# Four graph layers: from eight barriered blocks to one program per engine

## What is computed

```python
h = x
h = h + multi_head_graph_attention(h, adj)      # layer 0, 8 heads, masked softmax
h = layernorm(h); h = h + elu(graph_attention(h, adj))   # layer 1, 1 head
h = layernorm(h); h = h + relu(adj_sum(gated(h)))        # layer 2, relational
h = layernorm(h); h = h + attention(h, adj) @ Wo.T + bo  # layer 3, 4 heads
out = layernorm(h)

def layernorm(x, eps=1e-05):
    m = mean(x); v = var(x)
    return (x - m) / sqrt(v + eps)
```

## Time and profile before

| | |
|---|---|
| time, median of 3 runs | 827.31 (826.11 to 828.08) |
| profiled execution | 827.92, of which span 822.1 |
| busy share of the span | PE 85%, VectorE 75%, ScalarE 68%, GpSimd 49% |
| mean granted TensorE clock | 0.955 of full speed |
| layers, first to last work | 20 to 293, 300 to 433, 440 to 546, 551 to 814 |
| table loads from layer 0 on | 7, of 1.28 each |
| GpSimd's loads of the adjacency | median 3.0 from issue to landing |

### The profile page before, as it was taken

One profiled execution on the slowest core, in us unless ns is written; L12 is line 12 of the kernel. 1 busy time (PEld: TensorE's weight loads), 2 busy tenths in 40 slices (PEclk: granted clock), 3 DMA queues, 4 the chain that ended last, 5 costly groups with the idle time before them and its releaser, 6 DMA issues. The chain is left out here.

```text
span 822.1 us, 26183 instructions
## 1 busy us (share of the span) xinstructions
PE 700.0 (85%) x8450; PEld 517.3 (63%) x8482; DVE 616.0 (75%) x1758; ACT 560.4 (68%) x1266; POOL 399.7 (49%) x615
## 2 busy tenths in 40 slices
PE   5589999999998728999964999959999999999982
PEld 3366666666666416676744999946666666666751
DVE  4158878888788727999984788874777787778765
ACT  1346666656665449999955999945777777877871
POOL 0447787787778422545431111103455545545540
PEclk9999999999999959999986999978999999999995
DMA  1514333333332011232311333310222222222211
GB/s 47 147 47 98 79 83 96 94 72 90 96 71 46 16 27 21 38 38 32 39 13 52 91 81 86 90 28 11 48 46 51 57 45 53 56 57 45 53 47 39
DMA packets 34919, 47.76 MB, mean 58 GB/s; under 512 B 4394, under 2 KB 18484, under 8 KB 34868
## 3 DMA queue, kind: packets, MB, share of 16 engines
q0 software_dynamic: 18576, 21.01, 16.1%
q1 hardware_dynamic: 16292, 26.10, 10.1%
HBM read 51.33 MB, written 8.39 MB: 73 GB/s over the span
## 5 line engine op out<-in xcount | busy, mean ns | idle before, releaser
L490 DVE SCALAR_TENSOR_TENSOR pp<-banks,floor,adj 128x1024 f32<-128x1024 f32 x128 | 157.3, 1249 | 2.9 <-PE banks L585 2.5
L1113 POOL TENSOR_TENSOR pp<-pp,adj 128x512 f32<-128x512 f32 x64 | 73.5, 1166 | 121.5 <-ACT pp L1154 121.5
L416 ACT COPY rows<-banks 128x640 bf16<-128x640 bf16 x64 | 44.3, 692 | 69.4 <-PE banks L562 69.2
L1154 ACT ACTIVATE pp<-banks,nobound 128x512 f32<-128x512 f32 x128 | 81.5, 696 | 3.8 <-PE banks L1336 2.1
L585 PE MATMUL banks<-pp,yv 128*17 128x128 f32 x2048 | 82.5, 280 | 1.5 <-DVE pp L490 1.4
L716 POOL TENSOR_TENSOR yres<-oo,x 128x512 f32 (+1 forms) x32 | 40.8, 1275 | 67.6 <-DVE oo L821 67.6
L572 PE MATMUL banks<-rows 32*128 32x128 bf16 x1024 | 51.5, 219 | 22.2 <-DVE pp L490 20.6
L1032 PE MATMUL banks<-w2b,xt 128*128 128x256 f32 x256 | 61.8, 385 | 0.0
L340 POOL TENSOR_TENSOR yv<-wh,yv 128x512 f32<-128x512 f32 x32 | 35.2, 1099 | 52.1 <-ACT yv L409 52.1
L916 POOL DMA_DIRECT2D adj<-in_adj x32 | 17.0, 533 | 85.1 <-ACT sq L951 74.1
L421 ACT COPY ot<-banks 128x512 f32<-128x512 f32 x64 | 37.4, 584 | 29.4 <-PE banks L585 29.4
(11 more groups left out here) (219 smaller groups left out, 1953.7 us busy)
## 6 DMA issues: line engine op xcount, KB each, us to landing
adj<-in_adjt POOLq DMA_DIRECT2D x96, 128.0 KB, 3.0
xt<-in_xt SPq DMA_DIRECT2D x32, 256.0 KB, 3.8
x<-in_x SPq DMA_DIRECT2D x32, 256.0 KB, 3.2
adj<-in_adj POOLq DMA_DIRECT2D x32, 256.0 KB, 3.0
out_ngd<-yres SPq DMA_DIRECT2D x32, 256.0 KB
w3q<-in_wq SPq DMA_DIRECT2D x1, 64.0 KB, 1.8
w3k<-in_wk SPq DMA_DIRECT2D x1, 64.0 KB, 2.2
ident<-in_ident SPq DMA_DIRECT2D x1, 64.0 KB
```

Source lines behind the costliest of these rows:

```text
L416: nc.scalar.copy(rows[:, slot % 2, a, :], R[:, 0:5 * N]).then_inc(s["rw"], 1)
L490: nc.vector.scalar_tensor_tensor(pp[:, g], S[g % 2][:, :].rearrange("p (h n) -> p h n", n=N), floor[:, slot:slot + 1], adj[:, slot, g:g + ...
L1113: nc.gpsimd.tensor_tensor(pp[:, slot % 2, h], pp[:, slot % 2, h], adj[:, slot], ALU.mult).then_inc(s["pm"], 1)
L1154: nc.scalar.activation(pp[:, slot % 2, h], S[h][:, :], ACT.Exp, bias=k["nobound"][:, :], scale=SCALE).then_inc(s["p"], 1)
```

## The change

The functions of the four layers and `verdict` no longer open blocks. They return their programs (`Programs`), and a new function `layers` joins them into one program per engine inside one block and one phase. Semaphores are then taken for all of it: 135 in one clearing at the end, where each layer had its own (42, 23, 14 and 35) and each `row_statistics` and `verdict` 3.

`row_statistics` is gone. A class `Rows` does its work in two portions: portion 0 is graphs 0 to 119 (the first 30 portions of the batch), portion 1 the last 8 graphs. `variance` is the first seven VectorE operations as before. `roots` replaces square root and reciprocal by exp(-0.5 ln v) on ScalarE, and `refine` follows on VectorE with one Newton step and `nmr`. A layer's normalisations wait for `done` 1, those of its last two portions for `done` 2.

In layer 0 the table that holds both logarithm and exponential is named at the start, and it serves layer 1 too; it is named again at the end of layer 2 instead of at the start of layer 3.

Buffers of neighbouring layers lie in different parts of one area (`Plan`, 104 KB), except where a wait keeps them apart: `adj` of layer 1 lies over `xt` of layer 0, so GpSimd waits for layer 0's last projection (`projected`), and TensorE waits for layer 2's last `finish` before it writes a shared PSUM bank. GpSimd's last divide and addition of layer 0 stand behind the first three `adj` loads of layer 1, and its last addition of layer 1 behind two loads of layer 2.

In the diff, the changes of indentation are left out.

```diff
+class Rows:
+    def __init__(self, nc, sb, sem, L, stats, cut):
...
+    def columns(self, portion):
+        return slice(0, self.cut) if portion == 0 else slice(self.cut, B)
+
+    def variance(self, dve, portion):
+        nc, c = self.nc, self.columns(portion)
+        me, ve, mo, vo = (self.stats[:, c, n] for n in (1, 2, 4, 5))
+        mean, d, v = self.mean[:, c], self.d[:, c], self.v[:, c]
+        nc.vector.tensor_tensor(mean, me, mo, ALU.add).then_inc(self.link, 1)
+        nc.vector.tensor_tensor(d, me, mo, ALU.subtract).then_inc(self.link, 1)
+        nc.vector.tensor_tensor(v, ve, vo, ALU.add).then_inc(self.link, 1)
+        dve.wait_ge(self.link, 8 * portion + 3)
+        nc.vector.tensor_scalar(mean, mean, 0.5, None, ALU.mult)
+        nc.vector.scalar_tensor_tensor(d, d, 0.25, d, ALU.mult, ALU.mult).then_inc(self.link, 1)
+        nc.vector.tensor_scalar(v, v, 1.0 / D, EPS, ALU.mult, ALU.add).then_inc(self.link, 1)
+        dve.wait_ge(self.link, 8 * portion + 5)
+        nc.vector.tensor_tensor(v, v, d, ALU.add).then_inc(self.var, 1)
+
+    def roots(self, act, portion):
+        nc, c = self.nc, self.columns(portion)
+        act.wait_ge(self.var, portion + 1)
+        nc.scalar.activation(self.rstd[:, c], self.v[:, c], ACT.Ln).then_inc(self.log, 1)
+        act.wait_ge(self.log, portion + 1)
+        nc.scalar.activation(self.rstd[:, c], self.rstd[:, c], ACT.Exp, scale=-0.5).then_inc(self.root, 1)
+
+    def refine(self, dve, portion):
+        nc, c = self.nc, self.columns(portion)
+        r, d, v = self.rstd[:, c], self.d[:, c], self.v[:, c]
+        dve.wait_ge(self.root, portion + 1)
+        nc.vector.scalar_tensor_tensor(d, r, -0.5, r, ALU.mult, ALU.mult).then_inc(self.link, 1)
...
+        nc.vector.tensor_tensor(d, d, v, ALU.mult).then_inc(self.link, 1)
...
+        nc.vector.scalar_tensor_tensor(r, d, 1.5, r, ALU.add, ALU.mult).then_inc(self.link, 1)
...
+        nc.vector.scalar_tensor_tensor(self.nmr[:, c], self.mean[:, c], -1.0, r, ALU.mult, ALU.mult).then_inc(self.done, 1)
...
+def multi(nc, sb, sem, pb, k, yres, stats, rall, after, x_ngd, xt_dgn, adjt):
+        nc.scalar.preload_act_table_set("natural_log_exp_and_others")
         for n in range(3):
             copy_we(n, 0, n)
...
         evac_turned(T - 1, (T - 1) % RING, 0)
+        after.roots(act, 0)
         evac_turned(T - 1, (T - 1) % RING, 1)
...
         steps(dve, step, end)
+        dve.wait_ge(s["stats"], T - 2)
+        after.variance(dve, 0)
         statistics(T - 2, (T - 2) % RING)
+        after.refine(dve, 0)
         invert(T - 1, (T - 1) % RING)
         statistics(T - 1, (T - 1) % RING)
+        dve.wait_ge(s["stats"], T)
+        after.variance(dve, 1)
...
-def row_statistics(nc, sb, sem, L, stats, mean, rstd, nmr=None):
...
+def single(nc, sb, sem, pb, k, yres, stats, before, after, rec, layer0, adjt):
+        pool.wait_ge(layer0.projected, 2 * T)
         for n in range(3):
             load_adj(n, n)
+        layer0.tail()
...
             def normalize(n, slot, first=0, last=NG):
                 if first == 0:
+                    if known(n):
+                        act.wait_ge(before.done, 1 if n < T - 2 else 2)
...
         row_exp(0, 0)
+        before.roots(act, 1)
         evac_xt(1, 1)
...
         elu(T - 1, (T - 1) % R8)
+        after.roots(act, 0)
...
         weights(0, 0, 0)
+        before.refine(dve, 1)
...
         steps(dve, step, end, R8)
+        dve.wait_ge(s["stats"], T - 2)
+        after.variance(dve, 0)
         elu(T - 1, (T - 1) % R8)
         statistics(T - 2, (T - 2) % R8)
+        after.refine(dve, 0)
+
+        def last():
             statistics(T - 1, (T - 1) % R8)
+            dve.wait_ge(s["stats"], T)
+            after.variance(dve, 1)
...
+def relational(nc, sb, sem, pb, k, yres, stats, before, after, adjbad, layer1, adj_mgn):
         load_adj(1, 1)
+        layer1.tail()
...
         evac_xt(1, 1)
+        before.roots(act, 1)
         tanh(0, 0)
...
         steps(act, step, 26, R8)
+        nc.scalar.preload_act_table_set("natural_log_exp_and_others")
+        after.roots(act, 0)
...
-        for n in range(3):
-            normalize(n, n)
+        normalize(0, 0)
+        layer1.last()
+        normalize(1, 1)
+        normalize(2, 2)
         values(0, 0)
+        before.refine(dve, 1)
 
         def step(t, slot, lap):
+            if known(t) and t == T - 1:
+                dve.wait_ge(s["stats"], T - 2)
+                after.variance(dve, 0)
...
+def heads(nc, sb, sem, pb, k, yres, stats, before, rsum, layer2, adjt, out_ngd):
-            nc.scalar.preload_act_table_set("natural_log_exp_and_others")
...
         evac_v(0, 0)
+        before.roots(act, 1)
...
         normalize(0, 0)
+        layer2.last()
         normalize(1, 1)
...
         normalize(2, 2)
+        before.refine(dve, 1)
...
         queries(0, 0)
+        pe.wait_ge(layer2.finished, T)
         keys(0, 0)
...
+def layers(nc, sb, sem, fast, pb, k, c, yres, stats, rall, rec1, adjbad, rsum, flag, out_ngd):
...
+    place0 = Plan(nc, base, [(0, 80 * KB)])
+    place1 = Plan(nc, base, [(0, 24 * KB), (80 * KB, 101 * KB)])
+    place2 = Plan(nc, base, [(24 * KB, 64 * KB)])
+    place3 = Plan(nc, base, [(0, 24 * KB), (64 * KB, 104 * KB)])
+    r0, r1, r2 = (Rows(nc, sb, sem, L, stats, (T - 2) * NG) for L in range(3))
...
+    with nc.Block() as block:
...
+        @block.vector
+        def _(dve):
+            l0.dve(dve)
+            l1.dve(dve)
+            l2.dve(dve)
+            l3.dve(dve)
+            end.dve(dve)
...
```

More of the change, by code:

```diff
@@ L46, in known, with sync, gpsimd, scalar @@
     return isinstance(t, int)
+class Programs:
+    def sync(self, f):
+        self.sp = f
+    def gpsimd(self, f):
+        self.pool = f
+    def scalar(self, f):
+        self.act = f
+    def vector(self, f):
+        self.dve = f
+    def tensor(self, f):
+        self.pe = f
+class Plan:
+    def __init__(self, nc, base, runs):
+        self.nc, self.runs = nc, [[base + a, base + b] for a, b in runs]
+    def __call__(self, name, shape, dt):
+        size = math.prod(shape[1:]) * (2 if dt == BF16 else 4)
+        size = (size + 31) // 32 * 32
+        run = next(r for r in self.runs if r[1] - r[0] >= size)
+        run[0] += size
+        return self.nc.alloc_sbuf_tensor_at(name, shape, dt, offset=run[0] - size)
@@ new lines, in relational, with _, load_adj, step @@
+    block = Programs()
+    block.finished = s["y_out"]
+    @block.gpsimd
+    def _(pool):
+        def load_adj(n, slot):
+            need(pool, s["o"], n - 3)
+            need(pool, s["check"], n - 3)
+            pool.dma_start(adj[:, slot % RING, :, :], adj_mgn[:, bass.ds(n * NG, NG), :]).then_inc(adj_in[slot % RING], 16)
+        load_adj(0, 0)
+        load_adj(1, 1)
+        layer1.tail()
+        def step(t, slot, lap):
+            if not known(t) or t + 2 < T:
+                load_adj(t + 2, (slot + 2) % R8)
+        steps(pool, step, 26, R8)
@@ L1063, in heads @@
+    return block
+def heads(nc, sb, sem, pb, k, yres, stats, before, rsum, layer2, adjt, out_ngd):
     H, E = 4, 32
@@ L1395 @@
+        steps(pe, step, 26)
+        project(T - 1, (T - 1) % RING)
+    return block
 class General:
@@ L1751, in _ @@
+            l1.dve(dve)
+            l2.dve(dve)
+            l3.dve(dve)
+            end.dve(dve)
         @block.tensor
         def _(pe):
-            pe.wait_ge(s["col"], 1)
-            nc.tensor.matmul(pb[0][0:1, 0:1], col[:, 0:1], k["onescol"][:, :], start=True, stop=True).then_inc(s["row"], 1)
+            l0.pe(pe)
+            l1.pe(pe)
+            l2.pe(pe)
+            l3.pe(pe)
+            end.pe(pe)
 class Banks:
```

1868 lines of the change are left out of this document (934 added, 934 removed).

## The result

The changed kernel takes **805.62** (median of 4 runs, 801.26 to 807.47), the kernel before beside it 826.71 (823.89 to 828.08): ratio 0.9742, 95% interval 0.9694 to 0.9789. The profiled execution took 806.27, its span 801.6; before they were 827.92 and 822.1. The span is 20.5 shorter, against 19.1 in the prediction's sum; the other 1.1 fell outside it (4.7 in place of 5.8).

What follows compares the result with a forecast made beforehand. It took the row work and barriers between layers, four pipelines end to end, as the bound. Gains 0.2 + 8.0 + 5.4 + 3.0 + 2.5 = 19.1 off 827.92 gave 808.8, median 0.6 lower: 808.2; range 803.5 to 812.5.

Steps and rivals of the forecast that it cites:

- Start: Start of layer 0: naming the logarithm's table early moves a load out of the chain, 0.2 gained (bounds 0 and 1.28).
- Layer 0 to 1: First border: first normalisation at 291.65 instead of 300.19, 8.5 gained, less 0.5 for roots(1) in ScalarE's queue, net 8.0.
- Layer 1 to 2: Second border: refinement held until GpSimd's addition ends at 433.6, done at 434.9; normalisation was at 440.31, 5.4 gained.
- Layer 2 to 3: Third border: variance(0) ahead of finish(30), first normalisation at 547.9 against 550.87, 3.0 gained.
- The end: Kernel's end: verdict starts 3.27 earlier, one clearing of all 135 semaphores costs 0.73 more, 2.5 gained.
- the clock did no better: Rival at the ramps: shorter gaps spare some of TensorE's lower clock level, at most 9.0 back; 805, chance 0.15.
- The second portion: Rival in layers 1 and 2: roots(1) or late normalisation halves reach TensorE, 2 to 4 come back; 811, chance 0.18.
- GpSimd's three load issues: Rival at the first border: `adj` issues delay the first portion or hold VectorE, 4 to 6 back; 813, chance 0.05.
- No loop fetched its code again: Rival in the loops: code refetched at each of 14 jumps back, 13 or 26 lost; 821 or 834, chance 0.03.

Runs made afterwards that it cites:

- before_filler: The kernel before, with unread matmuls in TensorE's gaps at its three borders: 820.23, ratio 0.991 to the kernel before.
- filler: The changed kernel with 8, 15 and 10 unread matmuls in TensorE's gaps between layers: 798.12.
- early: The changed kernel with the first portion one step smaller (116 graphs) in layers 1 and 2: 798.23.
- early_filler: The changed kernel with a first portion of 116 graphs in layers 1 and 2, plus 8, 7 and 7 unread matmuls in TensorE's gaps: 794.78.
- final: The changed kernel with smaller first portions, normalisations ahead of elu, unread matmuls at start, borders and layer 2's ramp, GpSimd's loads ahead of both additions: 791.85, ratio 0.954.
- blocks: The changed kernel with its two portions kept, but one block with its barrier for each layer and the verdict: 817.6.

## Why the prediction held, term by term

The predicted 808.2 lies 2.6 above the median, inside the range. The mechanism came about as written at all three borders and at the end. The terms:

- **Start**, 0.2: ScalarE's copy behind the table load stands at 30.73 for 30.96 in the earlier trace rows, and layer 0's end is 0.19 earlier (its addition at 286.04 for 286.24 in the earlier trace rows).
- **Layer 0 to 1**, 8.0 net: 9.1. The divide at the end of layer 1 stands at 419.75 for 429.05 in the earlier trace rows, 9.30 less the start's 0.19. Two sizes in the 8.5 were off. The hold of variance(0) cost 0.44 (0.80 for 0.36), which with the quicker handovers made the variance ready 0.25 sooner, and the refinement began directly behind the roots and not 0.2 later, so the normalisation came at 290.98 for 291.45. Then layer 1 took 0.61 more than before up to its last matmuls (from 290.98 to 417.65, before from 300.19 to 426.25). 0.35 of that is roots(1), read at its place (the copy behind it begins 0.93 after the exponential ahead of it, before 0.58), so the 0.5 taken for it was about right; the rest fits the ramp's lower clock (0.82 for 0.86). The last matmuls then ran at the higher level (1.13, before 1.90), and the divide came 0.70 sooner behind them. Those 0.7 of the 9.1 are luck of the clock.
- **Layer 1 to 2**, 5.4: 15.04 - 9.30 = 5.7. The places of hold, elu and second portion were as written; the refinement was held until GpSimd's addition ended and was done at 425.2. TensorE waited for ScalarE's copy at transposition(1), 1.12 as before, and not for VectorE.
- **Layer 2 to 3**, 3.0: the statistics of portion 29 began 14.5 earlier (527.76 for 542.24), the normalisation 17.7, so 3.2. Layer 2 gave back 0.6, tanh(0) 7.8 after its start for 7.3, since the clock rose later in the ramp.
- **The end**, 2.5: 2.6. The verdict's wait of 3.27 is gone; the clearing took 762 ns for 46, 0.72 more.
- **Outside the span**: 1.1, which no term had.

Sum in the span: 0.2 + 9.1 + 5.7 + 3.2 + 2.6, less 0.6, and 0.2 in layer 3: 20.4, which is the 20.5 but for rounding.

Of the rivals, the clock did no better in the profiled execution (28.6 at the lower level for 25.7), and by before_filler it is not the gain's cause; that it was worth 8.2 in the ramps is shown by filler, near the 9.0 of the prediction's upper bound. The second portion didn't show in this kernel. At the second border it does as soon as the first starts 4 earlier (early: tanh(0) 8.9 after it for 7.8); for layer 1, where the prediction said this of 3, no run moved it. GpSimd's three load issues at the first border (287.26 to 288.91) didn't hold `variance(0)`, whose later operations took 0.21 to 0.36 beside them. No loop fetched its code again (28 packets, 1249 ns). The barriers' hidden price was GpSimd's drain. In the kernel before it made the first two borders long, and not only the first, as the prediction's may suggest. At the third border, where GpSimd had long ended, VectorE waited 0.8.

At layer 1's end the Trainium skill bears on what held VectorE. The Trainium skill, page "SBUF — State Buffer", section "SBUF: two separate sides", says that VectorE's operations in a two-port mode, or with two SBUF inputs against a GpSimd operation that reads SBUF, and GpSimd's exclude each other for a whole instruction, whoever comes first. The rows agree for two inputs (1.44 for 0.36), and for GpSimd as the loser (1.68 for 1.27 beside an elu). A normalisation with one SBUF tensor as input was held as well (1.32 for 0.34); in which mode it ran, no row says, and the 2.41 of early_filler are longer than one addition. On the table load the trace decides again as in the prediction: in final tanh begins 0.01 behind the load's end, so the drain of some 1380 ns that the Trainium skill, page "ScalarE: Activation LUTs", section "What ACT_TABLE_LOAD costs", adds is not there.

## What to carry to other kernels

Between two pipelined stages, ask which part of the reduction the next stage needs first, and cut there; taking the barriers away gave only some three fifths of this gain. Each step by which the first portion moves forward brings the second nearer to the path, and then the order on the other engines decides (two loads between two additions, a table load behind the roots). A gap on TensorE costs twice, once as a gap and once in the ramp behind it: fill short gaps with unread matmuls, and compare ramps, not medians, while the clock's changes fall at random.

## What the runs showed of the hardware

- A VectorE tensor_scalar on one float32 SBUF tensor is held by a GpSimd addition as well: 1.32 for 0.34 in early_filler, 1.30 in early. The one behind it took 2.41 in early_filler and 0.33 in early, at the same place.
- BN_STATS isn't held: 0.86 to 0.87 beside an addition as without one.
- GpSimd's drain right behind an addition of 1.27 ends 4.0 after that addition's start, some 2.7 after its end (4005 and 3991 ns in the kernel before, 4003 in blocks).
- The same start of the same matmul stream was run at either clock level from one kernel to another (0.76 and 1.33 for the four L645), and where the level rises within a ramp moved the third round of layer 1 by 1.7 (blocks).
- Clearing 135 semaphores took 762 ns. From 42 to 135 that is 5.4 ns each, as the 5.5 from 3 to 42 before.
